# A selective-scan and FFN kernel: the gate's `(1 + tanh) * value` moves from VectorE to ScalarE and GpSimd

## The reference, cut to what matters

```python
x, gate = (proj[..., :D_IN], proj[..., D_IN:])          # proj = layernorm(hidden) @ W_in.T
x = silu(conv(x)); ts, Bm, Cm = rms(x @ W_x.T)          # split in three
dt = softplus(ts @ W_dt.T + b_dt)
state = state * exp(dt_t * A) + (dt_t * u_t) * B_t       # over 2048 tokens, 16 states per channel
y = einsum(state, C_t) + x * D
s = (y * silu(gate)) @ W_out.T
g = silu(ffn(xn))                                        # quantised gate, up and down products
out = hidden + s * g
```

## Time and profile before

| | us |
|---|---|
| median of three runs | 3034.5 (3032.97 to 3039.14) |
| profiled execution, its own time | 3033.94 |
| span in its trace | 3032.1 |
| busy PE / DVE / POOL / ACT over the span | 2781.1 / 2322.8 / 1894.3 / 1540.3 |
| first `inj` of the long block starts | 768.23 |
| gate slots (tanh L1080, first to last start) | 781.9 to 1253.6 |

### The profile page before, as it was taken

One profiled execution on the slowest core, in us unless ns is written; L12 is line 12 of the kernel. 1 busy time (PEld: TensorE's weight loads), 2 busy tenths in 40 slices (PEclk: granted clock), 3 DMA queues, 4 the chain that ended last, 5 costly groups with the idle time before them and its releaser, 6 DMA issues.

```text
span 3032.1 us, 42354 instructions
## 1 busy us (share of the span) xinstructions
PE 2781.1 (92%) x15432; PEld 1605.1 (53%) x15432; DVE 2322.8 (77%) x2464; ACT 1540.3 (51%) x2512; POOL 1894.3 (62%) x822
## 2 busy tenths in 40 slices
PE   3999996763799999999999999998999999899999
PEld 3455554321455555555555555555666666556644
DVE  6344554233799999988888888889899999999910
ACT  2222112465566666677777776765455455555400
POOL 0000000244788998888888887888677788899811
PEclk7999997655899999999999999998999999999999
DMA  3121113377545655444454544465445545766541
GB/s 114 58 71 62 62 62 91 128 270 275 182 155 176 192 156 168 148 134 154 128 154 126 159 133 146 132 204 159 130 127 146 145 136 143 240 181 182 152 122 63
DMA packets 349448, 436.95 MB, mean 144 GB/s; under 512 B 169312, under 2 KB 178912, under 8 KB 348416
## 3 DMA queue, kind: packets, MB, share of 16 engines
q1 hardware_dynamic: 349264, 434.54, 47.4%
HBM read 296.37 MB, written 138.10 MB: 143 GB/s over the span
## 4 chain that ended last, share of the span: by engine, by line
PE 44%; DVE 18%; issue 6%; DMA 4%; POOL 1%; ACT 1%; SPq 1%; DVEq 0%; POOLq 0%; ACTq 0%
DVE inj L1165 10%; PE turned L1353 9%; PE bank L1395 9%; PE bank L1397 9%; PE bank L1423 8%; DVE ysum L1183 6%; PE bank L1471 6%; PE back L1437 2%; DMA gs_s<-work 1%; PE bank L1406 1%; DVE work L1219 1%; DMA h_s<-work 1%; DMA work<-in_wout 1%; POOL inj L1301 1%; PE bank L1376 1%
## 5 line engine op out<-in xcount | busy, mean ns | idle before, releaser
L1301 POOL TENSOR_TENSOR inj<-dub,bb 128x2048 f32<-128x2048 f32 x256 | 1161.2, 4536 | 312.2 <-PE turned L1353 294.6
L1165 DVE TENSOR_TENSOR_SCAN inj<-decay,carry,inj 128x512 f32<-128x512 f32 x1024 | 1284.0, 1270 | 28.5 <-POOL inj L1301 17.3
L1018 ACT ACTIVATE decay<-dtb,aneg 128x512 f32<-128x512 f32 x1024 | 704.8, 688 | 716.1 <-DVE inj L1165 710.6
L1353 PE MATMUL turned<-ident,inj 128*128 128x128 f32 x4096 | 627.2, 276 | 35.9 <-DVE inj L1165 24.4
L1353 PEld LDWEIGHTS turned<-ident,inj 128*128 128x128 f32 x4096 | 503.6, 142 | 249.6 <-DVE inj L1165 77.3
L1183 DVE SCALAR_TENSOR_TENSOR ysum<-turned,cT,ysum 128x512 f32<-128x512 f32 x721 | 528.1, 733 | 116.5 <-PE turned L1353 115.3
L1395 PE MATMUL bank<-xx,work 128*128 128x512 f16 x1408 | 534.4, 380 | 0.6 <-ACT work L1031 0.6
L1397 PE MATMUL bank<-xx,work 128*128 128x512 f16 x1408 | 534.4, 380 | 0.0
L569 POOL TENSOR_TENSOR du<-mx,du 128x2048 f32<-128x2048 f32 x16 | 86.2, 5406 | 664.5 <-DVE mx L560 664.5
L1376 PE MATMUL bank<-xx,work 128*128 128x512 f16 x1536 | 375.4, 381 | 43.4 <-POOL work L1281 43.4
L1310 POOL TENSOR_TENSOR ysum<-ysum,work 128x512 f32<-128x512 f32 x239 | 305.8, 1280 | 10.5 <-ACT work L1056 10.5
(11 more groups left out here) (135 smaller groups left out, 2947.2 us busy)
## 6 DMA issues: line engine op xcount, KB each, us to landing
bb<-bt_s SPq DMA_DIRECT2D x128, 512.0 KB, 5.7
work<-in_gu_q SPq DMA_DIRECT2D x88, 256.0 KB, 3.0
h_s<-work SPq DMA_DIRECT2D x88, 256.0 KB, 3.5
u_s<-ub SPq DMA_DIRECT2D x16, 1024.0 KB, 5.0
du<-u_s SPq DMA_DIRECT2D x16, 1024.0 KB, 6.3
dt_s<-mx SPq DMA_DIRECT2D x16, 1024.0 KB, 5.6
du_s<-du SPq DMA_DIRECT2D x16, 1024.0 KB, 4.7
dtb<-dt_s SPq DMA_DIRECT2D x32, 512.0 KB, 8.8
```

The lines of the kernel that those rows point to most:

```text
L1018: act.activation(decay[j % 2][:, :], dtb[:, step % 2, j, :], ACT.Exp, scale=aneg[:, step % G * J + j, n:n + 1]).then_inc(s_dec, 1)
L1165: v.tensor_tensor_scan(inj[:, s % RING, j, :], decay[j % 2][:, :], inj[:, s % RING, j, :], carry[:, step % G * J + j, n:n + 1], ALU.mult, ...
L1301: pool.tensor_tensor(inj[:, e % RING, :, :], dub[:, step % 2, :, :], bb[:, e % 8:e % 8 + 1, :].broadcast_to([P, J, T]), ALU.mult).then_inc ...
L1353: mm = pe.transpose(turned[t % 2][:, j * P:(j + 1) * P], inj[:, s % RING, j, t * P:(t + 1) * P], ident[:, :])
```

## The change

In the gate slots ScalarE does two more operations behind the tanh: it copies `bank[u % 3]` to `gout` (new L1084), and adds 1 to `ex` in place (new L1086). GpSimd multiplies `gout` by `ex` in place (new L1290), in its iteration e = u + 3, behind `gate_low` and ahead of inj(e). VectorE's operation L1219 is gone. The waits for the first `z_lo` and for `z_st` move from VectorE to the ScalarE copy. `z_ex` now counts three for each unit, and GpSimd waits for the third. `z_g` is raised by GpSimd.

```diff
@@ ScalarE, slot s, u = s - 1
                             act.activation(ex[:, :], bank[u % 3][:, :], ACT.Tanh, scale=0.5 / WS).then_inc(z_ex, 1)
+                            if u == 0:
+                                act.wait_ge(z_lo, LEAD + 2)
+                            atleast(act, z_st[u % 2], u // 2 * 16)
+                            act.activation(gout[:, u % 2, :], bank[u % 3][:, :], ACT.Copy).then_inc(z_ex, 1)
+                            act.wait_ge(z_ex, LEAD + 3 * u + 1)
+                            act.activation(ex[:, :], ex[:, :], ACT.Copy, bias=1.0).then_inc(z_ex, 1)
@@ VectorE, slot s, between scan(s, 1) and the second sum
-                        if 0 <= u < GATES:
-                            v.wait_ge(z_ex, LEAD + u + 1)
-                            if u == 0:
-                                v.wait_ge(z_lo, LEAD + 2)
-                            atleast(v, z_st[u % 2], u // 2 * 16)
-                            v.scalar_tensor_tensor(gout[:, u % 2, :], ex[:, :], 1.0, bank[u % 3][:, :],
-                                                   ALU.add, ALU.mult).then_inc(z_g, 1)
@@ GpSimd, iteration e
                             gate_low(half, gr[:, :])
+                        u = e - 3
+                        if 0 <= u < GATES:
+                            pool.wait_ge(z_ex, LEAD + 3 * u + 3)
+                            pool.tensor_tensor(gout[:, u % 2, :], gout[:, u % 2, :], ex[:, :], ALU.mult
+                                               ).then_inc(z_g, 1)
```

## The result

| | us |
|---|---|
| before, median (4 runs) | 3035.07 (3032.97 to 3039.14) |
| changed, median (4 runs) | 3313.08 (3310.64 to 3315.82) |
| ratio | 1.0916, 95% interval 1.0903 to 1.0929 |
| predicted | 3226, range 3140 to 3280 |
| inj(5) to inj(65), before / changed / predicted | 446.9 / 715.3 / 634 |

The change costs 278 us where 192 were forecast. The direction was right, the size was outside the range. The loss lies where it was placed: inj(65) starts 275.7 us later than in rows 11, and the span is 280.8 us longer.

The account below looks back on a forecast made before the run. VectorE was taken to bound the gate slots. The store's chain makes inj(5) to inj(65) 634 us instead of 446.9 (+187); with head, tail and clock +192 on the 3034.5 median gives 3226 us, range 3140 to 3280.

Parts of the forecast that it names:

- What bounds before: Gate slots before the change: VectorE sets the pace at 7.45 us a slot, TensorE 3% behind, at least 7.03.
- The store's chain: Gate slots, odd u: inj(u + 2), store landing, copy, add and product precede inj(u + 3); 20.8 us per two slots, against 14.9.
- The even unit does not add: Second half of each pair: ScalarE ends its add at 13.6 us, before GpSimd asks at 15.1; no extra time.
- the 13.6 us that I added for L1329: GpSimd, gate slots: 11 gate multiplications between inj(u + 3) and the next product, 1.24 us each, added to the span.
- The head and the tail: Ends of the gate stretch: inj(5) starts 6.7 us later, at 802.4; turn(64, 0) starts at 1450.7, +190.5.
- The 0.1 us for waking two engines: ScalarE's copy and add after the store lands: 2 x 0.65 plus this 0.1, together 1.4 us.
- The clock: TensorE in gate slots: dips after pauses, only the last costs, some 1.5 us; rival of 1.2 GHz throughout: 3436, chance 0.04.
- GpSimd's throughput alone: Rival, gate slots: the chain does not close and GpSimd runs without pause, 473 us; 3066 in all, chance 0.07.
- The short landing: Rival, gate slots: the chain holds but stores land in 3.5 us; 84 us less, 3142, chance 0.06.
- The other rule that I weighed: Gate slots: GpSimd's 64 new products could hold up VectorE's scans by up to 1.24 us each; priced at nothing.
- 0.6 us for the even unit: Upper end of the range: an extra 0.6 us for a pair that waits for the even unit too, up to 3280.
- if GpSimd is found waiting in front of even units too: Profile sign, GpSimd in gate slots: seeing such waits would make the forecast wrong; they were expected in every second iteration.

## Why the prediction was wrong

*What bounds before* held. With VectorE freed the slots went at TensorE's 7.02 us (7.03 worked out), and nothing more was to be had.

*The store's chain* held in mechanism and size. Its half of the pair took 13.6 us (13.8 forecast); the 32 stores behind a load were taken at 6.2 us, and this pair shows 6.2. Without the second loop and the third edge it gave 571 us for 28 pairs, where its terms make 579.

*The step that failed* is the sentence "The even unit does not add". I followed what the product of unit u + 1 needs (store, tanh, copy, add) and found ScalarE ready at 13.6 us, GpSimd at 15.1. I left out what stands in ScalarE's queue ahead of that tanh: L1056, which waits for the sum in GpSimd's iteration u + 3. That sum stands behind inj(u + 3), and by the prediction's own terms it ends at 15.1. So ScalarE was ready 3.7 us behind 15.1, not at 13.6. In the pair shown above it ends at 846.44, which is 14.8 us behind the end of inj(7), and the product waits for 3.66. My description of the kernel says that ScalarE weighs the fourth sum and GpSimd adds it; that the tile between them has one buffer, and so ties ScalarE's slot s to inj(s + 2), I did not write down. Before the change this wait was harmless. In slots 2 to 64 inj(s + 2) ended 2.2 to 4.3 us before L1056 of slot s started, and its sum takes 1.24. In slot 5 inj(7) ended at 815.19 and its sum at 816.42 (rows 4), and ScalarE, which had not waited for it, came to L1056 at 818.04:

```profile
818.04 0.67 ACT L1056 ACTIVATE work<-turned,cT 128x512 f32<-128x512 f32 x1
```

The same omission was made once more for the high half of the gated result, which costs some 4 us in every fourth slot (663.7 - 618.7 = 45 us between the two kernels with two buffers, over 11 such slots). The changed kernel hides it under L1056's wait, and for the same reason the 13.6 us that I added for L1329 were not paid.

In the sum: 27 pairs took 24.3 in the mean instead of 20.8, 95 us more. The three pairs at the begin of a step took 19.5, 18.1 and 21.5, together 59.1 where 3 x 20.8 - 3.7 = 58.7 were forecast. A sum is missing in them, and with it one of the new waits. The 13.6 us of L1329 were not paid. That leaves 81: 715 instead of 634.

*The head and the tail.* Inj(5) was forecast at 802.4 and started at 802.92. Part of that agreement is luck: the first `inj` of the block started 1.3 us later than before (769.53 against 768.23), and from there to inj(5) the change cost 6.0 us, not 6.7. From inj(65) to the end the kernel takes 1794.7 us against 1789.6, 5 more, where the forecast's own numbers (192 in all, 194 at inj(65)) had 2 less. The same stretch varies by 11 us over the twelve traces, so these 7 us are not resolved. One sum was off by 0.3: 1436 + 5.0 + 6.2 is 1447.2, not 1447.5. The 0.1 us for waking two engines stood on no row; copy, add and that together took 1.2 instead of 1.4.

*The clock* had little effect, as forecast. The 1437 gate matmuls between inj(5) and inj(65) took 419 ns in the mean instead of 379, and TensorE was busy with them for 398 us instead of 350, but both loops run through SyncE, ScalarE and GpSimd. In the kernel with two buffers and the early multiplication the granted clock was 0.89 in this stretch, and its pairs came out no longer than the sum, which holds no clock term. A run at another clock was not made.

*The rivals.* GpSimd's throughput alone (3066) was not what happened, but it is what the change costs once the order is mended: 3064.8. The short landing fell: the median of all 64 stores is 5.9 us (5.8 before), though the traffic fell from 162 to 103 GB/s. "DMA: Bandwidth & Descriptors" of the Trainium skill, section on the anatomy of one DMA, gives 2.0 us plus bytes over 436 GB/s for the GpSimd path. Carried over to SyncE's store behind its load that was an estimate of 3.8 us; with 6.2 in the pair shown, the trace of after differs from it as that of before does. The other rule that I weighed, "SBUF — State Buffer", section "Who interferes with whom", was misapplied: it speaks of VectorE instructions with two inputs in SBUF, and I said so of the scans, but `decay` is one of the PSUM tiles (the program takes it from the same allocator as `bank`). The 1.267 us of rows 10 therefore say nothing for or against that rule, and no run here tests it. It had no term in the sum.

*The range* was too narrow on one side. It was built from the spread of one term, the landing, and 0.6 us for the even unit, while a chain of waits that I had found in one place could have further members. My own list of signs named it ("if GpSimd is found waiting in front of even units too").

## What to carry to other kernels

When an instruction with a late input is put ahead of a periodic one in a queue, list every wait of every other engine on that queue, the ones that cost nothing today above all: here four of them (a store behind a load, a tile with one buffer, a high half, a load of `dq` behind a load of `bb`) had each been covered, or nearly, by the queue's lead. The same instruction behind the periodic one cost 30 us instead of 278. And an engine with 50 us of rest can take 50 us of work at most; a quarter of the units was worth moving, all of them were not.

## What the runs showed of the hardware

In one pair of the changed kernel the granted clock stood at 1.00 through a pause of TensorE of 4 us and fell when work resumed. Two-microsecond stretches, columns as in rows 1:

```profile
1006.00:1008.00 2.00, 1.75 (x10) 0.77 (x8) 1.56 (x2) 0.00 (x0) 2.00 (x1) 1.00 0.00 0
1008.00:1010.00 2.00, 0.00 (x0) 0.00 (x0) 0.00 (x0) 0.00 (x0) 2.00 (x2) 1.00 0.00 0
1010.00:1012.00 2.00, 0.30 (x3) 0.30 (x4) 0.00 (x0) 1.04 (x2) 2.00 (x2) 1.00 0.00 0
1012.00:1014.00 2.00, 2.00 (x9) 0.83 (x8) 1.74 (x2) 2.00 (x6) 0.08 (x1) 0.54 0.03 8
1014.00:1016.00 2.00, 2.00 (x9) 1.29 (x8) 1.57 (x3) 1.97 (x4) 0.95 (x1) 0.61 0.00 0
1016.00:1018.00 2.00, 2.00 (x13) 1.17 (x12) 1.79 (x2) 2.00 (x4) 2.00 (x2) 1.00 0.00 0
```

The rows of the timeline at the two ends of pauses in this pair, the idle time in brackets:

```profile
1011.70 0.73 PE L1357 MATMUL turned<-ident,inj 128*128 128x128 f32 x4 [3.95 <-ACT work L1056]
...
1022.86 0.66 PE L1357 MATMUL turned<-ident,inj 128*128 128x128 f32 x4 [2.33 <-ACT work L1056]
```
```profile
1022.00:1024.00 2.00, 1.14 (x8) 0.78 (x9) 0.58 (x1) 1.88 (x4) 2.00 (x3) 1.00 0.82 178
```

After the 3.95 us the clock was 0.54 and 0.61 in two stretches, which is some 3.4 us at the lower level of 1.2 GHz (0.50); after the 2.33 us it stayed at 1.00. But the length of the pause does not decide this alone. In an earlier pair the clock fell after a pause of 2.29 us:

```profile
847.27 0.66 PE L1357 MATMUL turned<-ident,inj 128*128 128x128 f32 x4 [2.29 <-ACT work L1056]
```
```profile
848.00:850.00 2.00, 2.00 (x7) 0.92 (x6) 2.00 (x3) 2.00 (x5) 0.00 (x0) 0.58 0.00 0
850.00:852.00 2.00, 2.00 (x9) 1.14 (x8) 1.83 (x3) 1.97 (x5) 1.90 (x2) 0.57 0.00 0
```

Nor did it always wait for work to resume: between 984 and 986 us TensorE did nothing, and the mean was 0.71.

```profile
984.00:986.00 2.00, 0.00 (x0) 0.00 (x0) 0.66 (x1) 2.00 (x4) 1.20 (x1) 0.71 1.06 380
```

Over the gate slots the mean is 0.90.
